# Gated cross-attention and a mixture of experts on one core: the second keys' scaling, the first load of x and the first read-back are moved

## The chip, the core and the metric

The kernel runs on one core of a Trainium2 chip. The metric is the device time of one execution in microseconds; the median of three runs is compared. TensorE (PE in the profile) multiplies, with its weight loads shown apart (PEld); VectorE (DVE), ScalarE (ACT) and GpSimd (POOL) work on tiles; SyncE (SP) only issues transfers here, and ACT and POOL issue some.

## The reference, cut to what matters

```python
# x: (16, 100, 512), ctx: (16, 361, 512), 32 heads of 16; D = 512
q = rmsnorm(heads(layernorm(x) @ Wq.T))          # rmsnorm over the 16 numbers of a head
k, v = split(ctx @ Wk.T, ctx @ Wv.T);  k = rmsnorm(k)
x = x + tanh(g_xattn) * softmax(q @ k.T * 0.25) @ v
h = layernorm(x)
top, id = top_1(h @ router_w.T)                  # 8 experts
routed = silu_mul((h * sigmoid(top)) @ w_gate_up[id]) @ w_down[id]     # F = 1024
shared = silu_mul(h @ shared_gate_up) @ shared_down
out = x + tanh(g_ffn) * (routed + shared)
```

## The kernel before, in words

Every engine runs one list of instructions, and semaphores tie the lists together. Attention is written out by hand in slots: a batch takes 24 slots, and each engine's function (`pe_attention`, `act_attention`, `dve_attention`, `pool_attention`) goes through the slots and issues what tables at the top of the file place there. A slot is about 1.35 us long.

While batch b is scored (`scoring`), a later one is prepared (`preparing`). Preparing has four row tiles: 0, 1 and 2 are the first, second and third 128 context rows (the third has 105), 3 is the 100 queries. For each, 12 matmuls make the keys or queries (L399; single-precision factors are split in a high and a low part, hence three products). ACT copies them (L558) and squares them (L560), DVE sums the squares per head (L742), takes the reciprocal root in ten small steps (`dve_rms`: L752, then L674 to L679) and scales (`dve_scale`, L765). ACT then writes the half-precision high part (L590), POOL the low part (`pack_low`, L771), TensorE transposes (L412), ACT copies back (L601). `RMS_SLOTS` has the slots of the roots: 16 for the first and second keys together, 19 for the queries, 27 for the third keys. `PACK_SLOTS` has the slot of the scaling for tiles 0 to 3; ACT's high part is one slot later and POOL's low part two. In a slot DVE does the roots first, then the scalings. Before the change the second keys (tile 1) are scaled in slot 21 and the queries in slot 22.

For scoring, TensorE makes the scores of a unit (L432), ACT the exponential (L608), TensorE the weighted values (L447) and, twice a batch, the transposes of the outputs (L459), which DVE finishes (L783, L786, L791 into `x_all`).

x comes in parts, given by `X_PARTS`; the layer norm of a part is statistics (L711), aggregates (L716) and a ten-step root. The first part, two batches, is made before all else on DVE; the low parts of the weights (L685) and of the context (L728) stand behind it. ACT makes their high parts (L521, L543).

At slot 361 the routing of chunk 0 (the first four batches) starts inside attention. In its step 13 POOL calls `pool_reload` (L1050): chunk 0 of x, which had been stored to `x1_rows` with one batch per column, is read back into `x_all` in tiles of 128 tokens. The other three chunks are routed and read back inside the shared expert, which starts when attention is over (`pe_shared`, L1209 gate and up, L1217 silu). The add of the shared expert's result (L1392) is what needs the rows read back. After it come the routed experts.

Of the kernel before, what the change touches and what calls it, by code (L numbers as in the profile page):

```python
# [47 lines left out]
RMS_SLOTS = (16, 19, 27)  # L48
RMS_TILES = (slice(0, 2), slice(3, 4), slice(2, 3))
RMS_OF = (0, 0, 2, 1)  # L50
PACK_SLOTS = (18, 21, 31, 22)
PACK_T_SLOTS = ((23,), (31,), (35,), (27, 29))
PACK_T_AT = (0, 3, 4, 1)

PV_SLOT = 2
X_PARTS = ((0, 2), (2, 4), (4, 8), (8, 12), (12, 16))
X_SLOTS = (None, -2, 22, 46, 70)
ROUTE_SLOT = 361
PAIR = ((0, 0), (0, 1), (1, 0))

# [1 line left out]
CT = 4  # L62
# [223 lines left out]
def prep_start(b):  # L286
    return 24 * (b - 2) + LEAD
# [333 lines left out]
def dve_attention(k):  # L621
    V, w = k.V, Waits(k.V)
    V.memset(k.bank[1][:, 0:GH * k.N], 0.0).then_inc(k.outs_cleared, 1)
    for s in range(k.first_slot, k.last_slot):
        for n in (n for n, at in enumerate(WEIGHT_SLOTS) if prep_start(0) + at == s):
            dve_weight_low(k, V, w, n)
        if s == prep_start(0) + 2:
            w.wait_ge(k.constants_made, 2)
            w.wait_ge(k.ident32_made, 2)
            V.tensor_copy(k.ident16[:], k.ident32[:]).then_inc(k.ident16_made, 1)  # L630
        if s == prep_start(0) + 16:
            w.wait_ge(k.constants_made, k.n_constants)
        for b, j in preparing(k, s):
            for p in range(4):
                if j == SRC_SLOTS[p] + 2:
                    dve_source_low(k, V, w, b, TILE[p])
        for c in range(len(X_PARTS)):
            if c:
                dve_layer_norm(k, V, w, 0, c, s - X_SLOTS[c])
            elif s == k.first_slot:  # L640
                for step in range(CT + 2):
                    dve_layer_norm(k, V, w, 0, 0, step)
        for b, i in scoring(k, s):
            for z in range(2):
                dve_finish(k, V, w, b, z, i - out_slots(k, b)[z] - 1)
        for b, j in preparing(k, s):
            if j == SRC_SLOTS[2] - 2:
                dve_normalise_x(k, V, w, b)
            for n in range(7):
                if j == taken_slot(n) + 1 and n not in VALUE_AT:  # L650
                    dve_sum_squares(k, V, w, b, PROJECTION_TILE[n])
            for g in range(3):
                if j == RMS_SLOTS[g]:
                    dve_rms(k, V, w, b, g)
            for t in range(4):
                if j == PACK_SLOTS[t]:
                    dve_scale(k, V, w, b, t)
        for c in range(4):
            dve_layer_norm(k, V, w, 1, c, s - 96 * (c + 1) - (22 if c < 3 else 6))
        if s == ROUTE_SLOT - 2:  # L660
            dve_router_zero(k, V, w)
        if s == ROUTE_SLOT - 1:
            dve_router_low(k, V, w)
        if 0 <= s - ROUTE_SLOT < ROUTE_STEPS:
            dve_route(k, V, w, 0, s - ROUTE_SLOT)
        if 0 <= s - ROUTE_SLOT - ROUTE_STEPS < 2:
            dve_part_low(k, k.first, V, w, s - ROUTE_SLOT - ROUTE_STEPS)
    return w
# [33 lines left out]
def dve_layer_norm(k, V, w, x1, c, step):  # L702

    first, end = ln_part(x1, c)
    before = ln_done(x1, c) - 1 - RSQRT_STEPS
    if 0 <= step < end - first:
        if x1:
            w.wait_ge(k.x1_made, 2 * end)
        else:
            w.wait_ge(k.x_in[c], 16)  # L710
        V.bn_stats(k.ln_raw[:, first + step, :], k.x_all[0:k.N, first + step, :]).then_inc(k.ln_v, 1)  # L711
    part = slice(first, end)
    if step == CT:
        w.wait_ge(k.ln_v, before - (end - first))
        for b in range(first, end):
            V.bn_aggr(k.ln_mv[:, b, :], k.ln_raw[:, b, :]).then_inc(k.ln_v, 1)  # L716
        w.wait_ge(k.ln_v, before)
        V.tensor_scalar(k.ln_var[:, part], k.ln_mv[:, part, 1], LN_EPS, None, ADD).then_inc(k.ln_v, 1)
    if step == CT + 1:
        for i in range(RSQRT_STEPS):  # L720
            w.wait_ge(k.ln_v, before + 1 + i)
            rsqrt_step(V, k.ln_rstd[:, part], k.ln_tmp[:, part], k.ln_var[:, part], i).then_inc(k.ln_v, 1)
# [14 lines left out]
def dve_sum_squares(k, V, w, b, t):  # L737
    rows = k.rows_of(t)
    w.wait_ge(k.squared, 4 * b + PLACE[t] + 1)
    if b >= 2:  # L740
        w.wait_ge(k.rms_v, 3 * RMS_EVENTS * (b - 1))
    V.tensor_reduce(k.sumsq[b % 2][0:rows, t, :], k.square[0:rows, :].rearrange("p (h d) -> p h d", d=HD),  # L742
                    AX.X, ADD).then_inc(k.summed, 1)
# [15 lines left out]
def dve_scale(k, V, w, b, t):  # L759
    rows, src, _, _ = pack_views(k, t)  # L760
    n = 4 * b + PLACE[t]
    w.wait_ge(k.rms_v, RMS_EVENTS * (3 * b + RMS_OF[t] + 1))
    w.wait_ge(k.raw_copied, n + 1)
    w.wait_ge(k.pack_low, n - 1)
    V.tensor_tensor(normed_view(k, t), src[0:rows].rearrange("p (h d) -> p h d", d=HD),  # L765
                    k.rms[b % 2][0:rows, t, :].unsqueeze(2).to_broadcast([rows, k.H, HD]), MULT).then_inc(k.scaled, 1)
# [251 lines left out]
def pool_route(k, G, w, c, step):  # L1018
    b0 = CT * c
    for j in range(CT):  # L1020
        if step == CT + 7 + j // 2:
            t0 = k.N * (b0 + j)
            w.wait_ge(k.xs_made, CT * c + j + 1)
            G.dma_start(k.gated_rows[t0:t0 + k.N, :], k.rows[j][0:k.N, :]).then_inc(k.rows_out[j], 16)
    if step == CT + 9:
        pool_reload(k, G, w, c)
    if step == CT + 10:
        w.wait_ge(k.rt_small, ROUTE_V * (c + 1))
        w.wait_ge(k.lists_cleared, 16)
        for b in range(b0, b0 + CT):  # L1030
            G.indirect_dma_start(k.lists, bass.IndirectOffsetOnAxis(ap=k.slot[:, b:b + 1], axis=0),
                                 k.token_id[:, b:b + 1], None).then_inc(k.table_out, 16)
# [12 lines left out]
def pool_reload(k, G, w, c):  # L1045

    w.wait_ge(k.x1_out[c], 16)
    w.wait_ge(k.xs_made, k.tile0[c + 1])
    for rows, tokens, tiles in chunk_rows(k, c):
        G.dma_start(k.x_all[0:rows, tiles, :],  # L1050
                    k.x1_rows[tokens, :].rearrange("(t p) d -> p t d", p=rows)).then_inc(k.x1_back[c], 16)
# [34 lines left out]
def sp_load_context(k, SP, w, b, tiles=slice(0, None)):  # L1086
    if b >= 2:
        w.wait_ge(k.src_low, 4 * (b - 1))
    keys = slice(P * (tiles.start or 0), P * tiles.stop if tiles.stop else k.M)
    n = 2 if tiles.start else b % 2  # L1090
    SP.dma_start(k.ctx_raw[b % 2][:, :, keys], k.ctxT[b][:, :, keys]).then_inc(k.ctx_in[n], 16)


def sp_load_x(k, SP, c):
    part = slice(*X_PARTS[c])
    SP.dma_start(k.x_all[0:k.N, part, :], k.x[part].rearrange("b n d -> n b d")).then_inc(k.x_in[c], 16)
# [8 lines left out]
def sp_attention(k):  # L1105
    SP, w = k.SP, Waits(k.SP)
    sp_load_x(k, SP, 0)
    sp_load_weights(k, SP, w, 0, 0)
    sp_load_context(k, SP, w, 0, slice(0, 1))
    sp_load_weights(k, SP, w, 0, 1)  # L1110
    for half in range(2):
        sp_load_weights(k, SP, w, 1, half)
    sp_load_context(k, SP, w, 0, slice(1, None))
    for half in range(2):
        sp_load_weights(k, SP, w, 2, half)
    sp_load_context(k, SP, w, 1)
    for c in range(1, len(X_PARTS)):
        sp_load_x(k, SP, c)
    for b in range(2, k.B):
        if b >= 2 * CT and b % CT == 0:  # L1120
            sp_store_x1(k, SP, w, b // CT - 2)
        sp_load_context(k, SP, w, b)
    sp_store_x1(k, SP, w, k.NCH - 2)

    w.wait_ge(k.projected, 7 * k.B)
    w.wait_ge(k.summed, 4 * k.B)
    w.wait_ge(k.scaled, 4 * k.B)
    for part in range(2):
        sp_load_part(k, k.first, SP, w, part)
    w.wait_ge(k.moe_constants, k.n_moe_constants)  # L1130
    SP.dma_start(k.rows[0][0:k.E, :], k.w_router).then_inc(k.router_in, 16)
    return w
# [133 lines left out]
def shared_points(it):  # L1266

    return 8 * it - 4 if it else 0
# [139 lines left out]
def pool_shared(k, G, w):  # L1408
    r = k.first
    w.wait_ge(k.x1_made, 2 * k.B)  # L1410
    for point in range(shared_points(16)):
        for chunk, step in route_at(point):
            pool_route(k, G, w, chunk, step)
    w.wait_ge(k.xs_made, k.B)
    w.wait_ge(k.x1_out[-1], 16)
    for t in k.y_rows:
        G.memset(t[:], 0.0).then_inc(k.y_cleared, 1)
    pool_gather(k, r, G, w, 0)
# [325 lines left out]
```

## Time and profile before

| what | value |
|---|---|
| median of 3 runs | 1075.78 us (1075.28 to 1075.85) |
| the profiled execution, its own time | 1080.07 us |
| its span, first to last instruction | 1078.0 us |
| TensorE busy | 1032.0 us |
| DVE, ACT, POOL busy | 629.8, 572.0, 175.4 us |
| mean granted TensorE clock | 0.982 |

Busy time is added up over the whole span; it does not say which engine a stretch waits for. The profiled execution took 4.3 us more than the median, so durations of the trace are compared with its own time.

### The profile page before, as it was taken

The page shows a single profiled execution, that of the slowest core. Times are in us where ns is not written, and L with a number is a line of the kernel's source. Part 1 is how long each engine was busy: PE and PEld are TensorE (multiplying, and loading weights), DVE is VectorE, ACT ScalarE, POOL GpSimd, SP SyncE. Part 2 cuts the span into 40 slices and gives each one's busy share as a digit, 9 for nine tenths or more (in the row PEclk, how much of TensorE's full clock was granted, in tenths as well). Part 3 has the DMA queues.
Part 4 walks back from the last instruction along what each step waited for, and adds up shares of the span by engine and source line. Part 5 has one row for each costly group of instructions (what it writes and reads, how often), then busy time and mean ns, then how long its engine had stood idle before and what let it go on. Part 6 is the DMA issues. An engine that isn't in the chain of part 4 may idle for free. (4 is left out here: it accounts for less than half of the span.)

```text
span 1078.0 us, 26800 instructions
## 1 busy us (share of the span) xinstructions
PE 1032.0 (96%) x11609; PEld 852.0 (79%) x11609; DVE 629.8 (58%) x1537; ACT 572.0 (53%) x865; POOL 175.4 (16%) x179
## 2 busy tenths in 40 slices
PE   5999999999999999999869999999999999999997
PEld 4677777777777777777649889999999999999996
DVE  4667674666456566474546654434357676667663
ACT  4576676776676776676632221212135555555552
POOL 1111101111101111101321430000001212233211
PEclk9999999999999999999779999999999999999999
DMA  7200000100001000100125330101148767777662
GB/s 246 76 30 30 29 30 30 33 29 30 30 30 61 2 30 30 47 14 2 44 62 154 114 104 20 40 20 40 50 135 255 224 214 226 238 226 236 211 203 73
DMA packets 64740, 99.68 MB, mean 92 GB/s; under 512 B 5548, under 2 KB 43436, under 8 KB 64618
## 3 DMA queue, kind: packets, MB, share of 16 engines
q1 hardware_dynamic: 55194, 78.18, 23.3%
q0 software_dynamic: 6544, 16.46, 5.1%
q10 hardware_dynamic: 2880, 3.29, 0.9%
q8 instruction: 93, 1.52, 0.6%
q14 instruction: 29, 0.24, 0.1%
HBM read 85.52 MB, written 13.56 MB: 92 GB/s over the span
## 5 line engine op out<-in xcount | busy, mean ns | idle before, releaser
L399 PE MATMUL bank<-arena_f32r 128*128 128x512 f32 (+2 forms) x1344 | 353.1, 407 | 11.9 <-DVE arena_f32r L728 11.7
L399 PEld LDWEIGHTS bank<-arena_f32r 128*128 128x128 f32 (+2 forms) x1344 | 231.9, 182 | 74.5 <-DVE arena_f32r L685 12.3
L608 ACT ACTIVATE probs<-score_banks 128x1600 f32<-128x1600 f32 x96 | 144.8, 1508 | 71.3 <-PE score_banks L432 66.8
L1227 ACT ACTIVATE hT_hi<-arena_f 128x224 fp32r<-128x224 f32 (+2 forms) x96 | 42.3, 440 | 167.0 <-DVE arena_f L1234 164.7
L771 POOL TENSOR_TENSOR k_pack<-normed,k_pack 128x512 f16<-128x512 f32 (+1 forms) x48 | 55.8, 1163 | 432.3 <-ACT k_pack L590 432.3
L447 PE MATMUL bank<-probs,values 128*17 128x100 f32 (+1 forms) x3072 | 87.9, 257 | 11.4 <-ACT probs L608 11.4
L447 PEld LDWEIGHTS bank<-probs,values 128*17 128x17 f32 (+1 forms) x3072 | 64.7, 99 | 37.1 <-ACT probs L608 18.3
L1209 PE MATMUL bank<-arena_f32r 128*128 128x224 f32 (+1 forms) x672 | 92.7, 297 | 0.8 <-DVE heads_out L786 0.8
L1209 PEld LDWEIGHTS bank<-arena_f32r 128*128 128x128 f32 x672 | 90.3, 194 | 2.3 <-DVE heads_out L786 1.2
L742 DVE TENSOR_REDUCE sumsq<-arena_f 128x32 f32<-128x512 f32 (+1 forms) x64 | 43.9, 686 | 78.7 <-ACT arena_f L560 78.7
L1234 DVE TENSOR_TENSOR arena_f<-bank,arena_f 128x224 f32<-128x224 f32 (+2 forms) x96 | 43.1, 449 | 78.0 <-PE bank L1209 77.9
L1209 PE MATMUL bank<-arena_f32r,wgate_hi 128*128 128x224 f32 (+1 forms) x416 | 78.0, 285 | 0.0
L1209 PE MATMUL bank<-arena_f32r,wup_hi 128*128 128x224 f32 (+1 forms) x416 | 77.7, 285 | 0.0
L1217 ACT ACTIVATE arena_f<-bank 128x224 f32<-128x224 f32 (+2 forms) x96 | 38.3, 399 | 72.3 <-PE bank L1209 71.8
L728 DVE TENSOR_TENSOR arena_f32r<-arena_f,arena_f32r 128x512 fp32r<-128x512 f32 (+1 forms) x48 | 31.6, 658 | 75.2 <-ACT arena_f32r L543 75.2
L1209 PEld LDWEIGHTS bank<-arena_f32r,wgate_hi 128*128 128x128 f32 x416 | 66.3, 191 | 2.2
L1209 PEld LDWEIGHTS bank<-arena_f32r,wup_hi 128*128 128x128 f32 x416 | 65.1, 191 | 0.0
L1209 PE MATMUL bank<-arena_f32r,wup_lo 128*128 128x224 f32 (+1 forms) x208 | 59.2, 285 | 0.0
L1209 PE MATMUL bank<-arena_f32r,wgate_lo 128*128 128x224 f32 (+1 forms) x208 | 59.2, 285 | 0.0
L590 ACT ACTIVATE k_pack<-normed 128x512 f16<-128x512 f32 (+1 forms) x48 | 30.4, 634 | 52.9 <-DVE normed L765 52.9
L1249 PE MATMUL score_banks<-arena_f32r,hT_hi 128*128 128x512 f32 (+2 forms) x184 | 58.0, 396 | 0.0
L1249 PE MATMUL score_banks<-wdown_lo,hT_hi 128*112 128x512 f32 (+2 forms) x140 | 55.0, 393 | 0.0
(175 smaller groups left out, 1870.0 us busy)
## 6 DMA issues: line engine op xcount, KB each, us to landing
arena_f<-L_ffn_w_gate_up SPq DMA_DIRECT2D x32, 512.0 KB
w_raw<-L_ffn_w_gate_up SPq DMA_DIRECT2D x32, 512.0 KB
arena_f<-ctx SPq DMA_DIRECT2D x15, 722.0 KB, 4.1
w_raw<-L_ffn_w_down SPq DMA_DIRECT2D x16, 512.0 KB
arena_f<-L_ffn_w_down SPq DMA_DIRECT2D x16, 512.0 KB
x_rows<-x_all SPq DMA_DIRECT2D x4, 800.0 KB
gated_rows<-arena_f POOLq DMA_DIRECT2D x16, 200.0 KB, 2.7
x_all<-x_rows POOLq DMA_DIRECT2D x4, 768.0 KB
```

Source lines behind the costliest of these rows:

```text
L399: product = PE.matmul(bank[0:rows, :], k.srcT[PLACE[t] % 2][a][:, j, 0:rows], weight, start=(m == 0), stop=(m == 11))
L447: product = PE.matmul(k.bank[1][HW * j:HW * j + HD + 1, k.N * r:k.N * r + k.N], k.values[b % 3][0:m, t, 16 * z + GH * r + j, :], k.probs[n ...
L590: A.activation(high[0:rows], src if t < k.NMT else src.to_broadcast([rows, k.H, 2, HD]), ACT.Copy).then_inc(k.pack_high, 1)
L608: A.activation(k.probs[n % 2][:], k.score_banks[:, :, 0:GH * k.N].rearrange("p j (r n) -> p j r n", r=GH), ACT.Exp, scale=float(HD) ** -0. ...
L728: V.tensor_tensor(low, src, high.bitcast(F32), SUB).then_inc(k.src_low, 1)
L742: V.tensor_reduce(k.sumsq[b % 2][0:rows, t, :], k.square[0:rows, :].rearrange("p (h d) -> p h d", d=HD), AX.X, ADD).then_inc(k.summed, 1)
L771: return engine.tensor_tensor(low[0:rows], normed_view(k, t), high[0:rows, :, 0, :], SUB)
L1209: made = PE.matmul(bank[:, 0:width], weight[a][:, i, P * j:P * j + P], xs[x][:, i, 0:width], start=(i == 0 and n == 0), stop=(i == k.KD - ...
L1217: A.activation(k.hidden[j][:, 0:width], k.bank[product_bank(r, it, j, 0)][:, 0:width], ACT.Silu).then_inc(r.silu, 1)
L1227: A.activation(k.hT[it % 2][0][:, j, 0:width], k.hidden[j][:, 0:width], ACT.Copy).then_inc(r.h_high, 1)
L1234: V.tensor_tensor(h, k.bank[product_bank(r, it, j, 1)][:, 0:width], h, MULT).then_inc(r.mult, 1)
L1249: made = PE.matmul(bank[0:rows, :], k.hT[it % 2][h][:, j, r0:r0 + rows], weight[a][:, j, :], start=(first and j == 0 and n == 0), stop=(la ...
```

## The change

Three things are moved. (1) The second keys are scaled in slot 19 instead of 21, and within a slot DVE does scalings ahead of roots, so this one stands in front of the root of the queries; ACT's and POOL's parts of tile 1 follow to slots 20 and 21. (2) The first part of x is one batch; the second batch is a part of its own, loaded behind the context of batch 0 and normed at slot 7 of batch 0. (3) Chunk 0 is read back by POOL behind its wait for the end of attention, no longer in step 13 of the routing.

```diff
-PACK_SLOTS = (18, 21, 31, 22)
+PACK_SLOTS = (18, 19, 31, 22)
-X_PARTS = ((0, 2), (2, 4), (4, 8), (8, 12), (12, 16))
-X_SLOTS = (None, -2, 22, 46, 70)
+X_PARTS = ((0, 1), (1, 2), (2, 4), (4, 8), (8, 12), (12, 16))
+X_SLOTS = (None, None, -2, 22, 46, 70)
...
         for c in range(len(X_PARTS)):
-            if c:
+            if c >= 2:
                 dve_layer_norm(k, V, w, 0, c, s - X_SLOTS[c])
-            elif s == k.first_slot:
+            elif s == (k.first_slot, prep_start(0) + 7)[c]:
                 for step in range(CT + 2):
-                    dve_layer_norm(k, V, w, 0, 0, step)
+                    dve_layer_norm(k, V, w, 0, c, step)
...
+            for t in range(4):
+                if j == PACK_SLOTS[t]:
+                    dve_scale(k, V, w, b, t)
             for g in range(3):
                 if j == RMS_SLOTS[g]:
                     dve_rms(k, V, w, b, g)
-            for t in range(4):
-                if j == PACK_SLOTS[t]:
-                    dve_scale(k, V, w, b, t)
...
-    if step == CT + 9:
+    if step == CT + 9 and c:
         pool_reload(k, G, w, c)
...
     sp_load_context(k, SP, w, 0, slice(1, None))
+    sp_load_x(k, SP, 1)
     for half in range(2):
         sp_load_weights(k, SP, w, 2, half)
     sp_load_context(k, SP, w, 1)
-    for c in range(1, len(X_PARTS)):
+    for c in range(2, len(X_PARTS)):
         sp_load_x(k, SP, c)
...
     w.wait_ge(k.x1_made, 2 * k.B)
+    pool_reload(k, G, w, 0)
     for point in range(shared_points(16)):
```

## Rows read from the trace of the kernel before

**Rows 1.** The page, busy us and share of the span of each engine.
```profile
PE 1032.0 (96%) x11609; PEld 852.0 (79%) x11609; DVE 629.8 (58%) x1537; ACT 572.0 (53%) x865; POOL 175.4 (16%) x179
```

**Rows 2.** Waits of TensorE, 60 to 500 us, then 0 to 60: total, times, longest.
```profile
PE bank L447 <- ACT probs L608: 4.6, 13, 0.4
...
PE bank L412 <- ACT kT L601: 2.3, 1, 2.3
```

**Rows 3.** Timeline of one batch: start, us, engine, line, operation, [idle before <-releaser].
```profile
255.74 0.17 DVE L752 TENSOR_SCALAR sumsq<-sumsq 128x32 f32<-128x32 f32 x1
255.96 1.16 POOL L771 TENSOR_TENSOR k_pack<-normed,k_pack 128x512 f16<-128x512 f32 x1 [14.66 <-ACT k_pack L590]
...
256.02 1.14 DVE L674 TENSOR_SCALAR rms<-sumsq 128x32 int32<-128x32 int32 x1
...
257.19 0.19 DVE L676 SCALAR_TENSOR_TENSOR rms_tmp<-rms 128x32 f32<-128x32 f32 x1
...
260.26 1.29 DVE L765 TENSOR_TENSOR normed<-arena_f,rms 128x512 f32<-128x512 f32 x2
...
260.98 0.63 ACT L590 ACTIVATE k_pack<-normed 128x512 f16<-128x512 f32 x1 [2.38 <-DVE normed L765]
...
261.58 1.06 ACT L590 ACTIVATE q_pack<-normed 100x1024 f16<-100x1024 f32 x1
261.68 1.16 POOL L771 TENSOR_TENSOR k_pack<-normed,k_pack 128x512 f16<-128x512 f32 x1 [4.56 <-ACT k_pack L590]
...
261.78 2.79 PE L399 MATMUL bank<-arena_f32r 128*128 128x512 f32 x11
...
262.80 1.17 POOL L771 TENSOR_TENSOR q_pack<-normed,q_pack 100x512 f16<-100x512 f32 x1
...
264.50 1.51 ACT L608 ACTIVATE probs<-score_banks 128x1600 f32<-128x1600 f32 x1
...
266.07 0.88 PE L447 MATMUL bank<-probs,values 128*17 128x100 f32 x32 [0.37 <-ACT probs L608]
```

**Rows 4.** Timeline, the stretched step of the first and of the last batch.
```profile
33.41 1.03 DVE L676 SCALAR_TENSOR_TENSOR rms_tmp<-rms 128x32 f32<-128x32 f32 x1
...
515.35 1.09 DVE L679 SCALAR_TENSOR_TENSOR rms<-rms_tmp,rms 128x32 f32<-128x32 f32 x1
```

**Rows 5.** Timeline of the start.
```profile
6.12 1.28 DVE L711 BATCH_NORM_STATS2 ln_raw<-x_all 100x6 f32<-100x512 f32 x2 [4.76 <-DMA x_all<-x]
7.18 1.06 ACT L521 ACTIVATE arena_f32r<-w_stage 128x1024 fp32r<-128x1024 f32 x1 [4.13 <-DMA w_stage<-L_xattn_Wv]
...
9.77 1.22 DVE L685 TENSOR_TENSOR arena_f32r<-w_stage,arena_f32r 128x1024 fp32r<-128x1024 f32 x1
...
11.05 1.06 ACT L521 ACTIVATE arena_f32r<-w_stage 128x1024 fp32r<-128x1024 f32 x1 [0.32 <-DMA w_stage<-L_xattn_Wk]
...
11.74 9.38 PE L399 MATMUL bank<-arena_f32r 128*128 128x512 f32 x28 [11.74 <-DVE arena_f32r L728]
12.36 1.06 ACT L521 ACTIVATE arena_f32r<-w_stage 128x1024 fp32r<-128x1024 f32 x1 [0.25 <-DMA w_stage<-L_xattn_Wk]
```

**Rows 6.** Timeline around the first read-back, in the last units of attention.
```profile
553.24 0.81 POOL L1050 DMA_DIRECT2D x_all<-x_rows  x1
...
553.84 1.99 ACT L1180 ACTIVATE arena_f32r<-arena_f 128x1024 fp32r<-128x1024 f32 x2
...
557.15 0.32 PE L432 MATMUL score_banks<-qT,kT 32*128 32x100 f16 x5 [0.50 <-issue]
...
560.31 1.50 ACT L608 ACTIVATE probs<-score_banks 128x1600 f32<-128x1600 f32 x1 [4.48 <-remote]
...
565.93 6.58 PE L1209 MATMUL bank<-arena_f32r 128*128 128x384 f32 x24 [0.81 <-DVE heads_out L786]
```

**Rows 7.** Timeline of ACT behind the third read-back.
```profile
615.18 0.53 ACT L1227 ACTIVATE hT_hi<-arena_f 128x384 fp32r<-128x384 f32 x1 [2.25 <-issue]
```

**Rows 8.** Windows: stretch, length, busy of PE, PEld, DVE, ACT, POOL, granted clock, DMA.
```profile
566.00:570.00 4.00, 4.00 (x13) 4.00 (x14) 3.79 (x13) 0.00 (x0) 0.00 (x0) 0.50 0.63 178
```

## The prediction

> **What bounds the kernel now.** I read the page first. TensorE is busy for 96% of the span [rows 1], so whatever holds TensorE up is paid for nearly one to one, and a faster ACT, DVE or POOL is worth only what it takes out of a TensorE wait. So the next view is the list of waits, cut to TensorE. Between 60 and 500 us it has one line of any size: the weighted values (L447) wait for the exponential on ACT (L608) 13 times, 0.4 us at most each [rows 2], about once a batch. Outside this stretch three places count: 11.7 us at the start, behind DVE [rows 5], 2.3 us in the first batch, where the transposes of the queries (L412) wait [rows 2], and near 560 us, where ACT begins L608 late [rows 6].
>
> The timeline of one batch, in the steady part, says where the 0.4 us come from [rows 3]. Follow it backwards. L447 starts at 266.07, when the exponential that started at 264.50 has ended. That exponential did not wait for TensorE: ACT reached it by running without a gap since the high part of the queries (L590 into q_pack) at 261.58. This high part stood behind the high part of the second keys (260.98 to 261.61) and behind DVE's two scalings (L765 x2), which end at 261.55. Those stand behind the ten steps of the queries' root on DVE, which begin with L674 at 256.02. And that L674, a step over 32 numbers a partition, took 1.14 us. POOL had started the low part of the first keys (L771) at 255.96 and held it to 257.12. The other steps take about 0.2 us. I looked at all 16 batches: in every one exactly one step of this root is stretched, to 1.03 to 1.15 us; it starts just after POOL's first L771 and ends with it [rows 4]. From the first of these steps to the last the batches are 32.1 us apart.
>
> So TensorE sits at the end of the chain: root of the queries, finish of an output (L783 to L791), scaling of the queries, high part, three copies and a square on ACT, exponential. Any delay of the scaling of the queries goes into TensorE's wait, as that wait is above zero already.
>
> **Part A: the second keys are scaled ahead of the queries' root.** It moves three instructions per batch: DVE's scaling of tile 1 (slot 21 to 19, and in front of the root), ACT's high part (slot 22 to 20), POOL's low part (slot 23 to 21). Nothing is removed. If the instructions did not disturb each other this would be worth nothing: DVE works without a break from 255.74 to 261.55 [rows 3], so the scaling ahead of the root pushes the root back by what it takes, 0.6 us (x2 took 1.29), and leaves out the same 0.6 us behind it. The high part of the queries would still start at 261.58.
>
> But they do disturb each other. Before, POOL's low part of the second keys ran at 261.68, when DVE had nothing to do. After, the scaling runs at 255.74 to 256.4, ACT (idle then, but for the copy of an output) makes the high part by about 257.1, and POOL's low part of the second keys is ready to run right behind that of the first keys. Two L771 back to back have a pitch of 1.12 us (261.68 and 262.80). So POOL is on its tiles from about 256.5 to 258.7, and DVE's root stands in that stretch. It is held up by two L771 instead of one: 1.12 us more. The bounds, per batch: if POOL's first L771 starts at 255.96 as it does now, even though DVE is in the scaling then, the two end at 258.25, L674 ends with them instead of at 257.16, so 1.09 us later, and 0.6 us of scaling less is behind it: +0.5 us. If L752 too gets stuck behind both, the whole root (L752 at 255.74 to L676 at 257.19 is 1.45 us, of which 0.28 between L752 and L674) begins at 258.7, and the sum is +1.4 us. The middle is that POOL waits for the scaling to end and DVE gets one or two steps in between: +1.1 us. I take this one, since DVE's root has a gap after each step, and in the rows POOL got in at once.
>
> Whether POOL waits for a DVE instruction that began first, no row shows. The Trainium skill says it does (SBUF — State Buffer, section Who interferes with whom: whichever of the two starts first gets the shared ports for the whole instruction, if DVE's reads two SBUF inputs and GpSimd's reads SBUF). By that rule a batch costs +1.1 us; without it, +0.5 us.
>
> Does TensorE see it? The high part of the queries would start at about 262.7, the exponential at 265.6, L447 at 267.2 instead of 266.07. The transposes of the queries (L412) would wait too, for POOL's low part, but this lies inside the same delay and is not added. Nothing behind TensorE's wait absorbs it: next comes TensorE's own work. So 16 batches by 1.1 us: **+17.6 us** (bounds 8 and 22). The first batch has the same order of work and a TensorE wait of 2.3 us at this place, the last the same stretched step, so I count both.
>
> **Part B: x for one batch, then one.** At the start DVE waits for x until 6.12, makes the statistics of two batches (x2, 1.28 us), their aggregates and a root, and only at 9.77 starts the low part of the first weights (L685), whose high part ACT had at 8.24. TensorE starts at 11.74 behind L685 and L728 [rows 5]. With one batch: half of the statistics less (0.6 us), some 0.1 us less of aggregates, and x lands earlier. Two 512 KB weight loads that ACT waits for come 1.31 us apart (11.05 and 12.36), so 200 KB are 0.5 us; this holds for x and for what is queued behind it. The sum is **-1.2 us** (bounds: 0.6 if x lands no earlier; 3.5 if TensorE, starting sooner, also gets its full clock sooner: its first 28 matmuls take 9.38 us, and at the 0.25 us of L399 in rows 3, 2.79 for 11, they would take 2.3 us less). The second batch's statistics, about 3 us, go to slot 7, where DVE only waits for the first square of the keys; the load of x for batch 1 goes past the three transfers ahead of it on SP's queue and stands in front of Wq, which ACT takes only at slot 12. Both are hidden; without that cover they would cost 3 us and 0.5 us.
>
> **Part C: chunk 0 is read back once attention is over.** POOL issues the reload (L1050, 768 KB) at 553.24. While it is under way TensorE's 32 score matmuls come in four pieces with pauses that no wait explains (0.50 us before the last, which ends at 557.47), and ACT starts the exponential at 560.31, 2.8 us after them, with nothing else to do [rows 6]. Behind L1180 it could have started at 555.83. That is 4.5 us on the path, and after it TensorE's granted clock is 0.50, the level of 1.2 GHz [rows 8]. Moved behind x1_made, the reload is issued near 566, when TensorE has its first 24 gate and up matmuls (6.58 us). I take **-4.5 us**. The bounds: -7.8 if the clock is up as well and halves these 6.58 us, 0 if the pause moves along: behind the third reload ACT has one of 2.25 us [rows 7], and behind the 24 matmuls TensorE needs ACT's silu. The first user of the rows read back is the add of the shared expert's first result, two chunks of matmuls later, so the reload is in time. POOL has nothing queued behind it until the routing of chunk 1. SP's store of x1 and weight loads share the transfer time there; ACT takes the first of those weights after the second chunk's silu.
>
> The Trainium skill speaks against part C: SBUF — State Buffer, section Who interferes with whom, says that a DMA never contends with a compute engine and that TensorE and ACT wait on nobody. By that rule part C is worth 0.
>
> **The sum.** +17.6 - 1.2 - 4.5 = +11.9 us. The profiled execution took 1080.07 us (span 1078.0 and 2.1 us around it), so 1092.0 us on its base; the median of the three runs is 1075.78, 4.3 us under it, and carried over: **1087.7 us**.
>
> **Rivals.**
> Rival 1, part A costs half: POOL's first low part starts in the middle of the scaling. 8 - 1.2 - 4.5 = +2.3 us, 1078.1. For it: no row shows POOL held up by DVE. Against: none shows a L771 beginning inside a DVE step of this length either. It would be slower by a little, or no change.
> Rival 2, nothing is gained by the reload, either because the pause moves to ACT's silu or because it belongs to the profiled execution alone: the profiled time is above the median by 4.3 us, about the size of the pause. +17.6 - 1.2 = +16.4, 1092.2. For it: rows 7 and this difference; against: the 28 matmuls of rows 5 run in one piece while the first loads come in.
> Rival 3, faster: POOL's second low part does not hold up the root. It is one mechanism: DVE's steps get through between or beside the two L771 so that the scaling of the queries is not later. Then A is 0, and the sum -5.7 us, 1070.1. It decides from the point where A costs under 0.36 us a batch. Against it: the step stretched to 1.1 us in 16 of 16 batches.
>
> **How the numbers follow.** About 0.2% (2.2 us) is what a measurement of this kernel can tell from no change. Chances: forecast 0.33, rival 1 0.14, rival 2 0.27, rival 3 0.26. Faster takes rival 3 but for a little, 0.25. Within 0.2% takes a part of rival 1, 0.07. Slower takes the rest, 0.68. The range must take in rival 3 and rival 2, as each holds more than 2 in 10: from 1069.5 to 1095, where the upper end is rival 2 with 1.3 us a batch. The forecast's own range is 1083 to 1092.
>
> **What would show it.** In the timeline after, L771 of the second keys begins within 0.2 us of the end of that of the first keys, and two DVE instructions, or one over 2 us, are stretched in each batch where one was. The scaling of the queries stands alone, and TensorE's waits at L412 and L447 are together 1 to 1.8 us a batch, not 0.4; the batches are 33.2 us apart, not 32.1. The first matmul starts at 10.5, not 11.74. The score matmuls of the last unit are in one piece, and L608 starts right behind them. I am wrong if the period stays at 32.1, which leaves only B and C; or if TensorE's clock falls to 1.2 GHz within the batches because of the longer waits, which would add to A beyond my range.

## The result, and the profile after

The kernel after takes 1088.76 us (median of 4 runs, 1088.22 to 1090.34), the kernel before beside it 1075.82 us: ratio 1.0119, 95% interval 1.0102 to 1.0137, so 11 to 15 us slower. The forecast was 1087.7 us, slower. The profiled execution took 1090.34 us (span 1088.4).

The page of the kernel after, busy us and share of the span:

```profile
PE 1033.2 (95%) x11609; PEld 853.5 (78%) x11609; DVE 645.8 (59%) x1548; ACT 570.6 (52%) x865; POOL 181.8 (17%) x179
```

Beside [rows 1] TensorE and ACT do the same work in the same time. DVE has 16.0 us more and POOL 6.4 us more. Part B's separate layer norm is some 3 us of DVE's (632.8 us in the run of B and C below); the rest is no more arithmetic, but instructions that took longer.

TensorE's waits from 60 to 510 us (total, times, longest), to be read beside [rows 2]:

```profile
PE bank L412 <- DVE heads_out L786: 18.2, 13, 1.4
PE bank L447 <- ACT probs L608: 0.5, 1, 0.5
```

The weighted values no longer wait. TensorE now waits 1.4 us a batch one step earlier, at the transposes of the first keys, for DVE's finish of an output (L786), as these transposes and the outputs share a bank. The timeline of the batch that [rows 3] show, in the kernel after:

```profile
258.96 0.69 DVE L765 TENSOR_TENSOR normed<-arena_f,rms 128x512 f32<-128x512 f32 x1
259.19 2.70 POOL L771 TENSOR_TENSOR k_pack<-normed,k_pack 128x512 f16<-128x512 f32 x2 [14.66 <-ACT k_pack L590]
259.57 0.17 DVE L752 TENSOR_SCALAR sumsq<-sumsq 128x32 f32<-128x32 f32 x1
...
259.85 0.96 DVE L674 TENSOR_SCALAR rms<-sumsq 128x32 int32<-128x32 int32 x1
...
260.84 1.10 DVE L676 SCALAR_TENSOR_TENSOR rms_tmp<-rms 128x32 f32<-128x32 f32 x1
...
263.95 0.42 DVE L786 TENSOR_TENSOR heads_out<-bank,inv_sum 100x256 f32<-100x256 f32 x1
...
264.52 0.61 PE L412 MATMUL bank<-ident,k_pack 128*128 128x128 f16 x8 [1.41 <-DVE heads_out L786]
264.82 0.69 DVE L765 TENSOR_TENSOR normed<-arena_f,rms 100x512 f32<-100x512 f32 x1
...
265.54 1.06 ACT L590 ACTIVATE q_pack<-normed 100x1024 f16<-100x1024 f32 x1 [2.95 <-DVE normed L765]
...
268.46 1.51 ACT L608 ACTIVATE probs<-score_banks 128x1600 f32<-128x1600 f32 x1
...
270.19 0.88 PE L447 MATMUL bank<-probs,values 128*17 128x100 f32 x32
```

Read down it: the second keys are scaled first, and POOL then has both low parts in one piece (x2). Two steps of the root are stretched, 0.96 and 1.10 us, where one was. Only behind the root comes the finish (L786), and TensorE has been standing for 1.41 us. From exponential to exponential the batches are 33.31 us apart in the steady part (mean of 12), against 32.41 before.

The start, to be read beside [rows 5]:

```profile
4.39 0.69 DVE L711 BATCH_NORM_STATS2 ln_raw<-x_all 100x6 f32<-100x512 f32 x1 [3.03 <-DMA x_all<-x]
...
7.47 1.23 DVE L685 TENSOR_TENSOR arena_f32r<-w_stage,arena_f32r 128x1024 fp32r<-128x1024 f32 x1
...
9.44 4.18 PE L399 MATMUL bank<-arena_f32r 128*128 128x512 f32 x9 [9.44 <-DVE arena_f32r L728]
```

x is there 1.7 us sooner, and the first matmul starts 2.3 us sooner. The end of attention, to be read beside [rows 6] (x_all is now read back at 578.16):

```profile
570.88 0.85 PE L432 MATMUL score_banks<-qT,kT 32*128 32x100 f16 x32
...
571.78 1.50 ACT L608 ACTIVATE probs<-score_banks 128x1600 f32<-128x1600 f32 x1 [0.53 <-PE score_banks L432]
573.34 1.53 PE L447 MATMUL bank<-probs,values 105*17 105x100 f32 x32 [1.61 <-ACT probs L608]
...
578.16 0.85 POOL L1050 DMA_DIRECT2D x_all<-x_rows  x1 [5.74 <-DVE x_all L791]
```

The last scores are in one piece and the exponential stands right behind them, as forecast. But the score and value matmuls take 0.85 and 1.53 us where the same ones take 0.53 and 0.88 at full clock. Windows of the last 50 us before ACT's first silu, kernel after and then kernel before (stretch, length, busy of PE, PEld, DVE, ACT, POOL, granted clock, DMA):

```profile
531.40:556.40 25.00, 19.24 (x382) 15.52 (x371) 9.76 (x29) 14.88 (x21) 5.86 (x15) 0.60 0.14 47
556.40:581.40 25.00, 19.77 (x288) 16.59 (x287) 13.11 (x49) 8.13 (x10) 7.76 (x9) 0.58 0.21 62
```

```profile
520.20:545.20 25.00, 19.42 (x370) 15.61 (x358) 9.58 (x28) 14.75 (x22) 6.97 (x16) 0.66 0.15 47
545.20:570.20 25.00, 15.03 (x280) 12.36 (x279) 13.20 (x51) 8.06 (x9) 7.45 (x9) 0.74 0.32 96
```

ACT's pause is gone, and the granted clock is lower (0.60 and 0.58, not 0.66 and 0.74; the level of 1.2 GHz is 0.5), so TensorE is busy 4.7 us longer in the second window with nearly the same matmuls (288 against 280 records). The silu comes 11.2 us later than before, nearly what the 85th exponential has lost already (10.5). In these two traces nothing of part C is left.

### The profile page after: what moved, and what is told of

It is laid out like the page before. It is cut to its first block and busy times, and to the rows that moved or that the text cites. A ratio compares the mean times of both kernels' runs of the same rounds, so it can differ in the third digit from the quotient of the medians.

```text
span 1088.4 us, 26813 instructions
## 1 busy us (share of the span) xinstructions
PE 1033.2 (95%) x11609; PEld 853.5 (78%) x11609; DVE 645.8 (59%) x1548; ACT 570.6 (52%) x865; POOL 181.8 (17%) x179
## 5 line engine op out<-in xcount | busy, mean ns | idle before, releaser
L771 POOL TENSOR_TENSOR k_pack<-normed,k_pack 128x512 f16<-128x512 f32 (+1 forms) x48 | 61.4, 1291 | 363.4 <-ACT k_pack L590 363.4
L447 PE MATMUL bank<-probs,values 128*17 128x100 f32 (+1 forms) x3072 | 89.2, 259 | 4.5 <-ACT probs L608 4.5
L447 PEld LDWEIGHTS bank<-probs,values 128*17 128x17 f32 (+1 forms) x3072 | 65.7, 100 | 29.8 <-issue 18.0
L742 DVE TENSOR_REDUCE sumsq<-arena_f 128x32 f32<-128x512 f32 (+1 forms) x64 | 43.9, 686 | 75.2 <-ACT arena_f L560 75.2
L1250 PE MATMUL score_banks<-wdown_hi,hT_hi 128*112 128x512 f32 (+2 forms) x140 | 54.9, 392 | 0.0
```

What stands on the lines that cost most here:

```text
L447: product = PE.matmul(k.bank[1][HW * j:HW * j + HD + 1, k.N * r:k.N * r + k.N], k.values[b % 3][0:m, t, 16 * z + GH * r + j, :], k.probs[n ...
L771: return engine.tensor_tensor(low[0:rows], normed_view(k, t), high[0:rows, :, 0, :], SUB)
L1250: made = PE.matmul(bank[0:rows, :], k.hT[it % 2][h][:, j, r0:r0 + rows], weight[a][:, j, :], start=(first and j == 0 and n == 0), stop=(la ...
```

## The experiments

Differences in us are the ratio less 1, times the median of the kernel before beside it. They can lie up to 1.2 us off the difference of the two medians. The kernel before is timed on each of the three chips.

**First question: what is each part worth alone?** Four kernels on one chip (before beside them 1079.2 us).

```diff
-PACK_SLOTS = (18, 21, 31, 22)
+PACK_SLOTS = (18, 19, 31, 22)     # and scalings ahead of roots in a slot
```

> Part A alone: the second keys scaled in slot 19 ahead of the queries' root; x and the read-back as before. Theory (GpSimd's two low parts in one row stand in the queries' root; 0.87 us a batch in the trace of the change): 16 x 0.87 = +14 us, 13 to 15. Rival (the other two parts brought some of the loss): under +11 us.

1095.03 us, ratio 1.0141 (1.0124 to 1.0159): +15.2 us. The batches are 33.31 us apart, the wait is the same (L412 behind L786, 18.3 us in 13 times from 60 to 510 us).

```diff
+X_PARTS = ((0, 1), (1, 2), (2, 4), (4, 8), (8, 12), (12, 16))     # nothing else of the change
```

> Part B alone: x loaded for one batch and then one. Theory (the 2.3 us by which the first matmul came earlier stay): -2 to -3 us. Rival (given back in the first batch, whose pack of the queries is what TensorE waits for): about 0.

1077.82 us, 0.9983 (0.9973 to 0.9993): -1.8 us. The first matmul starts at 9.52.

```diff
-    if step == CT + 9:
+    if step == CT + 9 and c:                # nothing else of the change
...
+    pool_reload(k, G, w, 0)                 # behind the wait for x1_made
```

> Part C alone: chunk 0 read back once attention is over. Theory of the prediction: the pause of 4.5 us goes, -4.5 us. Rival 2 (the pause is in the profiled execution alone, or comes again elsewhere): 0 within 1.5 us, and the profile of this run may still show the pause gone.

1076.47 us, 0.9972 (0.9962 to 0.9983): -3.0 us. But its profiled execution is no shorter than that of before (span 1077.7), and it has a pause of ACT of its own, with no read-back anywhere near. Timeline of this run:

```profile
555.48 1.50 ACT L608 ACTIVATE probs<-score_banks 128x1600 f32<-128x1600 f32 x1 [6.78 <-remote]
...
557.04 1.54 PE L447 MATMUL bank<-probs,values 128*17 128x100 f32 x32 [5.14 <-ACT probs L608]
```

ACT starts 3.6 us after the scores are there. The fourth kernel takes the kernel before and gives POOL one more low part of the first keys, into a spare tile, with nothing moved:

```diff
+                    if t == 0:
+                        rows, _, high, _ = pack_views(k, 0)
+                        G.tensor_tensor(k.pool_spare[0:rows], normed_view(k, 0), high[0:rows, :, 0, :], SUB)
```

> The kernel before with one more GpSimd instruction a batch: the low part of the first keys is also written to a spare tile, right before it is written to its place; the scaling of the second keys stays in slot 21. It prices a second GpSimd instruction inside the queries' root by itself. Theory (shared ports): a second step of the root is stretched to 1.1 us in every batch, TensorE waits at the transposes of the first keys for the finish of an output, +1.1 us x 16 = +14 to +18 us. Rival (the cost comes from the order of the scaling on DVE, 0.6 us ahead of the root): 0 to +2 us.

1092.07 us, 1.0121 (1.0102 to 1.0141): +13.1 us, and a batch every 33.33 us. Its timeline:

```profile
259.58 1.16 POOL L819 TENSOR_TENSOR pool_spare<-normed,k_pack 128x512 f16<-128x512 f32 x1 [14.66 <-ACT k_pack L592]
259.63 1.14 DVE L676 TENSOR_SCALAR rms<-sumsq 128x32 int32<-128x32 int32 x1
260.70 1.16 POOL L773 TENSOR_TENSOR k_pack<-normed,k_pack 128x512 f16<-128x512 f32 x1
260.81 1.10 DVE L678 SCALAR_TENSOR_TENSOR rms_tmp<-rms 128x32 f32<-128x32 f32 x1
```

So a second POOL instruction inside the root is enough for the period of the whole change. DVE stands at each nearly as long as POOL runs. TensorE waits at the transposes of the first keys for the finish here too (12.5 us in 13 times from 60 to 500 us), and its old wait for the exponential stays beside it (4.7 us).

**Second question: is it POOL, or the scaling that stands ahead of the root?** Four kernels on another chip (before 1075.66 us). The first is part A with POOL's low part of the second keys held until the queries' root is done:

```diff
+                    if t == 1:
+                        w.wait_ge(k.rms_v, RMS_EVENTS * (3 * b + RMS_OF[3] + 1))
```

> Part A, but GpSimd's low part of the second keys waits until the ten steps of the queries' root are done. The scaling stays ahead of the root. Theory (the second low part inside the root is most of the cost): what is left is the scaling's 0.6 us in front of the root, less the 0.37 us of a wait that it swallows, +0.2 to +0.5 us a batch, +4 to +8 us. Rival (the order of the scaling is the cost): +14 us as before.

1080.7 us, 1.0038 (1.0021 to 1.0054): +4.1 us, batches 32.68 us apart. TensorE still waits at L412 for L786, 6.3 us in 13 times, and 2.3 us at L447. Read in this order, 0.63 of part A's 0.90 us a batch are POOL's second low part inside the root, and 0.27 the scaling ahead of it. Read from the kernel with one more low part (33.33 us), the same scaling adds nothing (33.31): the two costs overlap, and how they split depends on which comes first. The second has the new slot, with roots ahead of scalings as before:

```diff
-PACK_SLOTS = (18, 21, 31, 22)
+PACK_SLOTS = (18, 19, 31, 22)     # the order within a slot is unchanged
```

> Slot 19 for the second keys, but the scaling behind the root instead of ahead of it. The second low part on GpSimd then falls on the finish of an output, whose two first instructions read PSUM. Theory: the finish is 0.6 us later, no second step of the root is stretched, +4 to +9 us. Rival (any earlier low part costs the same): +14 us.

1103.01 us, 1.0259 (1.0232 to 1.0285): +28 us, a miss of all expectations. The batches are 34.16 us apart, and TensorE waits 15.7 us in 13 times at L447 and 8.0 us in 12 times at L412 (60 to 500 us). A timeline of this run:

```profile
272.68 0.68 DVE L765 TENSOR_TENSOR normed<-arena_f,rms 128x512 f32<-128x512 f32 x1
...
273.40 0.63 ACT L590 ACTIVATE k_pack<-normed 128x512 f16<-128x512 f32 x1 [3.94 <-DVE normed L765]
...
274.11 1.42 POOL L771 TENSOR_TENSOR k_pack<-normed,k_pack 128x512 f16<-128x512 f32 x1 [3.41 <-ACT k_pack L590]
...
274.32 1.50 ACT L608 ACTIVATE probs<-score_banks 128x1600 f32<-128x1600 f32 x1
274.43 1.65 DVE L765 TENSOR_TENSOR normed<-arena_f,rms 100x512 f32<-100x512 f32 x1
...
275.87 1.50 PE L447 MATMUL bank<-probs,values 128*17 128x100 f32 x32 [1.12 <-ACT probs L608]
```

ACT runs its list in order and reaches the high part of the second keys before its scaling is done. It stands there for 3.9 us with a unit's exponential behind it. POOL's low part then falls on the scaling of the queries (1.65 us, not 0.69), and L447 runs at 1.2 GHz here (1.50 us, not 0.88): between 60 and 500 us the clock falls in four short stretches, which no other kernel shows. The clock is not the whole of it: the typical batch takes 33.80 us, 1.4 more than before. The third takes the other low part out, in the kernel before:

```diff
+                    if t == 0:      # the first keys' low part waits for the end of the queries' root
+                        w.wait_ge(k.rms_v, RMS_EVENTS * (3 * b + RMS_OF[3] + 1))
```

> The kernel before, with GpSimd's low part of the first keys held back until the queries' root is done, so that no step of the root is stretched. Theory: the root ends 0.95 us earlier, the queries are scaled some 0.4 us earlier, TensorE's wait of 0.37 us for the exponential goes: -4 to -6 us. Rival (the low part of the first keys is now late for its transposes, or falls on DVE's next two-input instruction): 0 or slower.

1068.3 us, 0.9943 (0.9925 to 0.9960): 6.1 us faster than before (4.3 to 8.1). Its timeline and its waits of TensorE from 60 to 500 us:

```profile
253.86 0.18 DVE L674 TENSOR_SCALAR rms<-sumsq 128x32 int32<-128x32 int32 x1
...
256.22 1.16 POOL L771 TENSOR_TENSOR k_pack<-normed,k_pack 128x512 f16<-128x512 f32 x1 [17.08 <-DVE rms L679]
...
256.74 0.92 DVE L791 SCALAR_TENSOR_TENSOR x_all<-heads_out,gates,x_all 100x256 f32<-100x256 f32 x1
```

```profile
PE bank L447 <- ACT probs L608: 0.6, 2, 0.4
PE bank L412 <- POOL k_pack L771: 0.4, 1, 0.4
```

No step of the root is stretched. POOL now stretches the second half of the finish (L791, 0.92 against 0.48 us), for which nobody waits. The period is 31.90 us, and the wait per batch is gone. The wait stood 13 times in the kernel before, and 13 times 0.51 us are 6.6 us, within the interval. The fourth is the whole change without part C:

```diff
-PACK_SLOTS = (18, 21, 31, 22)
+PACK_SLOTS = (18, 19, 31, 22)     # and scalings ahead of roots in a slot
+X_PARTS = ((0, 1), (1, 2), (2, 4), (4, 8), (8, 12), (12, 16))
```

> Parts A and B, the read-back at its old place. If the parts add up as measured alone (+15.2 and -1.8 us): +13.4 us. Rival (part C gains nothing behind a longer attention): the same as the whole change beside it, +12.9 us, and part C would then be worth 0 there.

1088.95 us, 1.0129 (1.0102 to 1.0156). Beside the whole change (1.0119) part C is worth 1 us here, within the intervals.

**Third question: does the best of it add up, and does the pause belong to the read-back?** Four kernels on a third chip (before 1075.22 us, median of 17). The first is parts B and C without A:

```diff
+X_PARTS = ((0, 1), (1, 2), (2, 4), (4, 8), (8, 12), (12, 16))
-    if step == CT + 9:
+    if step == CT + 9 and c:
+    pool_reload(k, G, w, 0)                 # behind the wait for x1_made
```

> Parts B and C without A. By the sum of the two runs alone -4.8 us, ratio 0.9955. If part C gives nothing where the first batch has started sooner, -1.8. With the whole change it says what part A is worth beside them: 13.1 + 4.8, about 18 us, if the parts add up; about 15 us, as A alone, if they don't. No step of the queries' root is stretched twice, the batches are 32.4 us apart.

1074.43 us, 0.9990 (0.9979 to 1.0001): -1.1 us, a miss against the sum of -4.8. The second is part B with the first keys' low part later:

```diff
+X_PARTS = ((0, 1), (1, 2), (2, 4), (4, 8), (8, 12), (12, 16))
+                    if t == 0:
+                        w.wait_ge(k.rms_v, RMS_EVENTS * (3 * b + RMS_OF[3] + 1))
```

> The same as the first of this call, with chunk 0 read back in step 13 of the routing as before. -8 to -9 us if the first two add up. The difference to the first of this call is what part C is worth where TensorE waits least: -3.0 us as alone, -1 as beside parts A and B, or 0 if its 3 us were the pause of ACT that comes and goes. If the read-back itself makes ACT's pause ahead of the last exponentials, the pause is here and not in the first.

1066.9 us, 0.9921 (0.9896 to 0.9946): -8.5 us, as the two add up (-7.9). The third is this kernel with part C as well:

```diff
-    if step == CT + 9:
+    if step == CT + 9 and c:
+    pool_reload(k, G, w, 0)                 # behind the wait for x1_made
```

> The version that the runs so far point to: x for one batch and then one, the read-back of chunk 0 once attention is over, the second keys' scaling left where it was before, and GpSimd's low part of the first keys behind the queries' root. If the three parts add up as they were timed one by one (-7, -1.8 and -3.0 us), it is -10 to -12 us against the kernel before, and the batches are 31.9 us apart. If the read-back is worth only the 1 us that it was worth beside the other two parts, it is -8 to -10. If the parts take the same waiting time of TensorE twice, it is no better than the low part alone, -6 to -7.

1065.59 us, 0.9906 (0.9890 to 0.9923): -10.1 us. This version is faster than both kernels. The batches are 31.91 us apart, with no wait at L412 or L447 over 0.4 us. Against the kernel without part C it gains 1.6 us, within the intervals. The fourth is the kernel before, unchanged, profiled a second time:

> The kernel before, unchanged, in a second profiled execution. If the read-back in step 13 makes the pause of ACT ahead of the last exponential (2.8 us behind its scores), the pause is there again, at the same unit. If the pause comes and goes by itself, as its presence in the run of part C alone suggests, it may be absent or stand at another unit; its absence alone would show that it isn't tied to the read-back.

1073.33 us, and the pause is not there, though the read-back is where it was. Timeline of this second execution of the kernel before:

```profile
549.35 1.50 ACT L608 ACTIVATE probs<-score_banks 128x1600 f32<-128x1600 f32 x1 [1.58 <-PE score_banks L432]
...
550.15 0.81 POOL L1050 DMA_DIRECT2D x_all<-x_rows  x1
...
552.65 1.49 ACT L608 ACTIVATE probs<-score_banks 128x1600 f32<-128x1600 f32 x1
```

The same kernel twice, with 6.8 us between the spans (1078.0 and 1071.2); whether both executions were on one chip is not known. The windows of its last 50 us before the silu:

```profile
512.50:537.50 25.00, 18.66 (x415) 14.15 (x417) 13.96 (x42) 17.03 (x25) 8.13 (x17) 0.85 0.15 48
537.50:562.50 25.00, 18.92 (x351) 16.23 (x344) 14.53 (x55) 9.46 (x10) 7.44 (x9) 0.77 0.35 80
```

Up to the 85th exponential it is 1.3 us ahead, at the silu 7.7: 6.3 us of one kernel's time come and go in the 69 us between the two, by the pause and by the clock (0.85 and 0.77 against 0.66 and 0.74).

## Why the forecast came out

**Part A, +17.6 us forecast, +15.2 measured alone (13.4 to 17.2), +13.9 as the whole change less the run of B and C.** The mechanism was right: the second low part of POOL falls into the queries' root and stretches a second step, in every batch, and an additional POOL instruction at the same place costs nearly the same without anything moved. One ladder of five kernels shows it, with the number of L771 inside the root:

| L771 inside the queries' root | kernel | us per batch |
|---|---|---|
| none | before, first low part later | 31.90 |
| one | before | 32.41 |
| two | before, one more low part | 33.33 |
| two | part A | 33.31 |
| one, scaling ahead | part A, second low part later | 32.68 |

POOL did wait for the end of the scaling, as the forecast's middle case had it. The size of the term was 1.1 us a batch; 0.90 was measured, so 16 batches are 14.4 us, not 17.6. Rival 1 (half of it) and rival 3 (none) are out. (The prediction's 32.1 us is the mean from the first batch to the last, and the first ones are shorter; in the steady part the period went from 32.41 to 33.31 us.) The term is smaller for two reasons that the rows show. The root itself grew by less than a full L771: from L752 to the end of the first L676 it takes 1.64 us before and 2.37 us after, 0.73 us more and not the 1.12 of a second L771. POOL's piece begins 0.38 us ahead of L752, under the scaling, and not 0.22 us behind the start of L752; less the 0.43 us that POOL stands still there, this takes 0.17 us off. The other 0.22 are the step L676 that DVE would have run anyway, and which is now the second one stretched. And TensorE had a wait of 0.37 us at this point of the batch, which the new one takes the place of (1.41 - 0.37 = 1.04, and 0.14 of that comes back elsewhere in the batch).

The place of the wait was wrong: the prediction had it at L447, and 18.2 of the 18.7 us stand at L412. The prediction held that the scaling ahead of the root costs nothing, since it leaves out as much behind it. That is true of the scaling of the queries, and not of what stands between: DVE's finish (L783 to L791) comes behind the root and ahead of the scalings. From the queries' sum of squares (L742) to L786 it is 5.47 us before and 6.79 after: 0.6 for the scaling and 0.73 for the stretched root. TensorE stands at the transposes of the first keys for it, and the later start of the exponential (0.73) lies inside this wait. The prediction named this finish in the chain and did not ask who waits for it. The run with the second low part held back prices it: 0.27 us a batch for the scaling ahead of the root, where only one low part stands in it.

**Part B, -1.2 forecast, -1.8 measured alone (-0.8 to -2.9).** The first matmul starts 2.3 us sooner, not 1.2. The term mis-sized is x's landing: 1.7 us sooner instead of the 0.5 that the pitch of the weight loads gave. In the run of B alone it is 1.8 (4.35 against 6.12). Why 200 KB less are worth so much at the start was not tried. As forecast, the second batch's statistics lie in DVE's idle time (15.48, 0.67 us). That less arrives at the end may be the clock of the first batches; the profiled executions scatter by more than this there (1.4 us between the two of before), so it is not shown.

**Part C, -4.5 forecast: this step failed.** The prediction took ACT's pause for the price of the read-back. The pause is there with the read-back moved away (part C alone, 3.6 us) and absent with it in its old place (before, second execution; the run of A and B). So it is not the price of the transfer one to one, which speaks for the second half of rival 2.

It is not shown either that the pause comes by chance with the execution. It goes with the chip: it stands in all four profiled executions on the chip of the first question, and in none of the eight on the other two. The kernel before takes 1079.2 us on that chip, and 1075.7 and 1075.2 us on the others, 3.5 and 4.0 us less, about as much as the pause. Of the first two profiled executions, before has the pause and after has not. No kernel is known to have been profiled twice on one chip, so chip and execution are not told apart.

What moving the read-back is worth is, by four pairs of runs, -3.0 (alone), +0.7 (beside B), -1.1 (beside A and B) and -1.6 us (beside B and the later low part), each uncertain by 1.1 to 3.5 us; the mean is -1.3, and none but the first differs from nothing. Only the first and the last pair were taken on one chip each, and the first is from the chip with the pause. Seven of the eight runs of part C alone took 1076.1 to 1077.1 us there; the eighth, profiled and with the pause, took 1079.64, and the 17 of before 1077.0 to 1082.2. So the read-back may still make the pause likelier on that chip. This and what makes the pause stay open. The Trainium skill (SBUF — State Buffer, section Who interferes with whom) says that a DMA never contends with a compute engine. The last three pairs agree with it within their intervals; for the -3.0 us of the first no run shows the cause.

**The sum.** By the runs it would be +15.2 - 1.8 - 1.3 = +12.1 us with the mean for part C, and +10.4 us with its -3.0 alone; the forecast was +11.9, and 11 to 15 were measured. So that the total came out was luck in part, as two errors offset each other: part A was taken 2.4 us too high and part C 1.5 to 3.2 us too good. Some of the 4.3 us by which the profiled execution stood above its median was probably the very pause that part C was credited with; the prediction said so in rival 2 and gave it 0.27. That deserved more, as a pause without a releaser in one execution is a single observation.

## What to carry to other kernels

Ahead of moving an instruction, look at what POOL runs at the same time as DVE's chains of small steps: here a step of 0.19 us became nearly as long as POOL's instruction (0.95 to 1.15 us), and one L771 of 1.16 us in a chain on the path was worth 0.5 to 0.9 us. One wait that moves POOL's work behind the chain gained 6 us here; the order that put more of it inside lost 15. When an instruction is pushed ahead of another on an in-order engine, price everything between its new and its old place, not only its own user. And a pause that stands once in one execution wants a second profile of the same kernel, on another chip too, before it goes into a sum.

## What the runs showed of the hardware that was not expected

- POOL is held up as well. In part A its L771 begins at 259.19 inside DVE's scaling (258.96 to 259.65), and two take 2.70 us instead of 2.28 (1.12 us pitch and 1.16). In the run with the second low part later one takes 1.59 instead of 1.16. In these rows whichever began first keeps going, and POOL gets the 0.43 us on top. The Trainium skill states this in the same section on interference, and the trace agrees.
- A gap of ACT between the scores and an exponential, with nothing in the profile to wait for, stands in 5 of the 14 profiled executions (2.4 to 3.6 us): before, A alone, B alone, C alone and the one more low part, the last four being all that were profiled on one chip. It is always at one of the last two units of attention, with the read-back at its old place or moved away; before's second execution is without it.
- The same kernel has spans of 1078.0 and 1071.2 us in two profiled executions; 6.3 us of the difference arise within 69 us at the end of attention, where TensorE has gaps and its granted clock changes between 1.2 and 2.4 GHz.
